# Expert pairs of a transformer layer: lags of 3, 6 and 9 steps in place of 2, 4 and 6

## The chip, the cores and the metric

The kernel runs on one core of one Trainium2 chip, as one program. The metric is device time in microseconds (us) from the start to the end of the program. A core has five engines with queues of their own: TensorE (PE; its weight loads are PEld), VectorE (DVE), ScalarE (ACT), GpSimd (POOL) and SyncE (SP), which here only issues DMAs. Engines meet at semaphores: an instruction raises a count, another waits for it.

## The reference

One layer on 8 sequences of 512 tokens, width 256, in float32. The routed part is computed densely in the reference; the kernel sorts tokens by expert.

```
x = x + attention(layernorm(x))          # 16 query heads, 4 key heads, rotary, causal
h = layernorm(x)
logits = h @ gate_w.T                    # 64 experts
topv, topi = top_k(logits, 8);  rw = softmax(topv)
gate, up = split(h @ gu_w[e].T)          # 256 -> 2 x 64, for each expert e
out = sum over chosen e of  rw[e] * (silu(gate) * up) @ dp_w[e].T      # 64 -> 256
out = out + sigmoid(h @ sh_gate1_w.T) * ((silu(h @ sh_gate_w.T) * (h @ sh_up_w.T)) @ sh_down_w.T)
x = x + out
```

## The kernel before

The first stage makes attention, the second layernorm and the routing, and scatters every token's row to `rows_d` once for each of its 8 experts, so that the rows of an expert lie in blocks of 128 (320 blocks, the last never used). The second stage, which the change touches, takes the blocks in 160 pairs (`PAIRS`). It is software-pipelined by hand: each engine runs through one loop over `STEPS` steps, and in step i it does different stages of different pairs:

- SyncE loads the rows of a pair into `xg` (L1155), up to eight pairs ahead.
- TensorE turns the rows, `turn_x` (L1402, into PSUM `psA`); ScalarE copies them to `xT` (L1297).
- GATE steps later TensorE multiplies by the expert's gate and up weights, `gate_up` (L1412, `psB`), found by a register from the list of block owners; ScalarE makes silu of the gate half into `inner` (L1302) and VectorE multiplies the up half in (`gated`, L1216).
- TURN steps after its rows were turned, the pair's inner rows are turned, `turn_inner` (L1420, `psC`); ScalarE copies them to `innerT` (L1306).
- DOWN steps after, the down product, `down` (L1429, `psD`); ScalarE copies it to `y` (L1313) and GpSimd scatters its two blocks to `res_d` with two indirect DMAs (L1497), to the rows that VectorE has worked out in `dst_i` (`pick` and `destine`).

A step's order on TensorE is down, shared products, turn_inner, then a count up of `e_front`; gate_up, turn_x, then a count up of `e_back`. ScalarE's is y copy, innerT copy (both wait for `e_front` of that step), silu, xT copy (both wait for `e_back`). VectorE's is the product, then every second step the destinations of two pairs, then sums.

The buffers are rings: `xT`, `inner` and `innerT` hold A = 3 pairs, `xg` holds 16 blocks, `y` 10 blocks, `dst_i` 32 blocks, and each of psA to psD two pairs. `down` waits until psD's bank has been copied (`e_d`) and for its innerT (`e_c`); `gate_up` waits for xT (`e_a`), `turn_inner` for inner (`e_in`).

`SOONER` lists the steps of the first two pairs, which are not delayed by the full lag. Beside the pairs, each 128-token tile is summed over its 8 expert rows once all its blocks are scattered: SyncE waits for the scatters and loads `yk` and `xs` (`load_tile`, at a turn given by LOADED_BEFORE), VectorE adds from step `sum_step` on (SUMMED_AFTER), and TensorE, at fixed steps after `sum_step`, makes the shared expert. The last four tiles are summed after the loop, from loads that wait for the last scatter (L1174).

Of the kernel before, what the change touches and what calls it, by code (L numbers as in the profile page):

```python
# [56 lines left out]
def build(nc, x, const, wqkv, wo, wroute, wgu, wdp, wshd, out):  # L57
# [7 lines left out]
    with ExitStack() as top:  # L65
# [919 lines left out]
        with ExitStack() as ctx:  # L985
# [2 lines left out]
            held_back = sb("held_back", [P, EXPERTS * D], F32)  # L988
            PAIRS = BLOCKS // 2
            G, R, Y, A = 16, 4, 10, 3  # L990
            GATE, TURN, DOWN = 2, 4, 6
            xg = sb("xg", [P, G, ROW], F32)
            xT = sb("xT", [P, A, 2, KC, P], F32)
            inner = sb("inner", [P, A, 2, P], F32)
# [35 lines left out]
            res_v = res_d.rearrange("(t p k) h -> t p (k h)", p=P, k=TOP)  # L1030

            STEPS = PAIRS + DOWN + 4
            SOONER = {GATE: (1, 2), TURN: (2, 4), DOWN: (3, 6)}
            step_of = {stage: [SOONER[stage][i] if i < 2 else i + stage for i in range(PAIRS)] for stage in SOONER}

            def pairs_at(stage, step):

                return [i for i in range(PAIRS) if step_of[stage][i] == step]
            LOADED_BEFORE, SUMMED_AFTER = 26, 12
            SUM_STEPS, TURN_SHARED, DOWN_SHARED, MIX = 4, 2, 4, 5  # L1040


            def held_of(pair):

                return min(2, USED - 2 * pair)
# [331 lines left out]
            def _(pe):  # L1377
# [19 lines left out]
                def turn_x(i):  # L1397

                    pe.wait_ge(e_x[i % (G // 2)], 16 * (2 * i // G + 1))
                    for b in range(held_of(i)):  # L1400
                        for c in range(KC):
                            last = pe.transpose(psA[:, i % 2, (b * KC + c) * P:(b * KC + c + 1) * P],  # L1402
                                                xg[:, (2 * i + b) % G, c * P:(c + 1) * P], ident)
                    return last

                def gate_up(i):

                    pe.wait_ge(e_a, i + 1)
                    for b in range(held_of(i)):
                        off = offsets[2 * i + b]  # L1410
                        for c in range(KC):
                            last = pe.matmul(psB[:, i % 2, b * GU:(b + 1) * GU], xT[:, i % A, b, c, :],  # L1412
                                             wgu_s[:, bass.ds(off + c * GU, GU)], start=(c == 0), stop=(c == KC - 1))
                    return last

                def turn_inner(i):

                    pe.wait_ge(e_in, i + 1)
                    for b in range(held_of(i)):
                        last = pe.transpose(psC[:, i % 2, b * P:(b + 1) * P], inner[:, i % A, b, :], ident)  # L1420
                    return last
# [20 lines left out]
                for i in range(STEPS):  # L1442
                    if i % 2 == 0 and i < PAIRS:
                        load_offsets(2 * i)
                    for pair in pairs_at(DOWN, i):
                        last = down(pair)
                    for tile, s in tile_at(i):
                        if s == DOWN_SHARED:
                            pe.wait_ge(c_t, tile + 1)
                    for tile, s in tile_at(i - 1):  # L1450
                        if s == MIX:
                            pe.wait_ge(c_mix, tile + 1)
                    for tile, s in tile_at(i):
                        if s == TURN_SHARED:
                            last = turn_shared(tile)
                        if s == DOWN_SHARED:
                            last = down_shared(tile)
                    for pair in pairs_at(TURN, i):
                        last = turn_inner(pair)
                    if has_front(i):  # L1460
                        last.then_inc(e_front, 1)
                    for pair in pairs_at(GATE, i):
                        last = gate_up(pair)
                    if i < PAIRS:
                        last = turn_x(i)
                    if has_back(i):
                        last.then_inc(e_back, 1)
# [91 lines left out]
```

## Time and profile before

| what | value |
|---|---|
| median of 3 runs | 1210.2 us (1207.94 to 1212.99) |
| span of the profiled execution | 1382.2 us |
| its own time beside the span | the profile tells none |
| mean granted clock of TensorE | 0.909 of 2.4 GHz |
| TensorE, VectorE, ScalarE, GpSimd busy | 1080.5, 703.8, 647.6, 722.5 us |
| expert stage | about 809 to 1355 us of the span |

The profiled execution is slower than the others by 172.0 us; times inside it are on its own scale. In a row, a group of instructions is named by line, engine, operation, and what it writes and reads; "waited for" rows give the total wait, how many times, and the longest.

### The profile page before, as it was taken

The numbers are of one execution on the slowest core, as the hardware profiler recorded it, in microseconds if no ns is written. First come the engines' busy times: TensorE is split into PE (matmuls) and PEld (weight loads), VectorE is DVE, ScalarE is ACT, GpSimd is POOL, SyncE is SP. The second block draws the span as 40 slices with busy tenths as digits, with TensorE's granted clock in tenths as the row PEclk, the third lists the DMA queues.
The fourth block names the chain that finished last, engine by engine and source line by source line (L and its number), as shares of the span: only waits on it lengthen the run. The fifth ranks groups of instructions, "written<-read, shape, count | busy, mean of one in ns | idle before, by whom it ended". The sixth has DMA issues, their size and how long they took to land.

```text
span 1382.2 us, 23533 instructions
## 1 busy us (share of the span) xinstructions
PE 1080.5 (78%) x7305; PEld 833.1 (60%) x7305; DVE 703.8 (51%) x2197; ACT 647.6 (47%) x1586; POOL 722.5 (52%) x953
## 2 busy tenths in 40 slices
PE   3799998888888888889765058887888878787875
PEld 1566666565565656566534047777777767676763
DVE  3476766666666666656525411121245544444447
ACT  2465656555555555655331024444445444444441
POOL 3111225657466564564566735655565565655552
PEclk9699999999999989989877569999999999998996
DMA  2586877212122121122228855555767777776536
GB/s 82 174 288 221 275 256 237 101 48 95 51 84 93 53 90 51 59 102 61 84 93 289 269 172 161 172 169 154 238 233 251 268 268 248 259 243 238 170 138 212
DMA packets 142824, 233.18 MB, mean 169 GB/s; under 512 B 17303, under 2 KB 119910, under 8 KB 137840
## 3 DMA queue, kind: packets, MB, share of 16 engines
q1 hardware_dynamic: 67936, 101.06, 22.7%
q0 software_dynamic: 27600, 69.28, 14.1%
q10 hardware_dynamic: 47168, 61.35, 13.5%
q8 instruction: 63, 1.03, 0.3%
q14 instruction: 57, 0.47, 0.1%
HBM read 107.32 MB, written 132.53 MB: 174 GB/s over the span
## 4 chain that ended last, share of the span: by engine, by line
PE 46%; DVE 16%; another core or an unknown queue 14%; issue 13%; ACT 8%; POOL 1%; DMA 1%; ACTq 0%; SPq 0%; DVEq 0%; POOLq 0%
PE psB L1412 6%; DVE nmax L868 6%; PE psD L1429 5%; PE psv L607 4%; PE ps L511 4%; PE psA L1402 4%; PE ps L558 3%; PE ps L518 3%; PE psp L490 3%; PE psp L504 3%; PE psC L1420 3%; ACT xT L1297 2%; ACT y L1313 2%; PE psq L634 2%
## 5 line engine op out<-in xcount | busy, mean ns | idle before, releaser
L1497 POOL DMA_INDIRECT res_d<-y,dst_i x319 | 320.9, 1006 | 231.9 <-ACT y L1313 117.8
L463 POOL DMA_INDIRECT rows_d<-pay,slot_i x256 | 256.5, 1002 | 75.4 <-issue 73.4
L868 DVE TENSOR_REDUCE nmax<-ps 128x1 f32<-128x512 f32 (+3 forms) x448 | 225.8, 531 | 135.8 <-PE ps L518 93.5
L736 ACT ACTIVATE wgu_s<-ps 128x512 f32<-128x512 f32 x320 | 191.9, 600 | 123.4 <-PE ps L518 91.3
L1216 DVE TENSOR_TENSOR inner<-inner,psB 128x128 f32<-128x128 f32 x160 | 45.8, 286 | 316.8 <-ACT inner L1302 250.5
L1429 PE MATMUL psD<-wdp_s,innerT 128*128 x638 | 174.8, 397 | 21.1 <-ACT innerT L1306 17.6
L1412 PE MATMUL psB<-wgu_s,xT 128*128 x1276 | 179.1, 285 | 1.2 <-ACT xT L1297 0.8
L518 PE MATMUL ps<-mask,ident_b 128*128 128x256 bf16 (+1 forms) x640 | 175.4, 274 | 0.4 <-issue 0.4
L511 PE MATMUL ps<-kT,qT 96*128 96x512 f32 (+3 forms) x512 | 168.3, 391 | 8.1 <-DVE nmax L868 4.8
L558 PE MATMUL ps<-qT,kT 128*128 128x512 f32 (+3 forms) x512 | 165.8, 387 | 4.9 <-ACT wgu_s L736 4.2
L1412 PEld LDWEIGHTS psB<-wgu_s,xT 128*128 128x128 f32 x1276 | 163.9, 201 | 1.8 <-issue 1.2
L1313 ACT COPY y<-psD 128x512 f32<-128x512 f32 x160 | 97.7, 610 | 110.1 <-PE psC L1420 53.7
L1402 PE MATMUL psA<-cst,xg 128*128 128x128 f32 x638 | 102.9, 284 | 55.2 <-DMA xg<-rows_d 51.2
L1429 PEld LDWEIGHTS psD<-wdp_s,innerT 128*128 128x128 f32 x638 | 113.7, 199 | 37.4 <-issue 27.9
L1302 ACT ACTIVATE inner<-psB 128x128 f32<-128x128 f32 x160 | 48.6, 304 | 176.9 <-remote 106.0
L1297 ACT COPY xT<-psA 128x512 f32<-128x512 f32 x160 | 97.6, 610 | 56.0 <-PE psA L1402 56.0
L1402 PEld LDWEIGHTS psA<-cst,xg 128*128 128x128 f32 x638 | 80.0, 148 | 57.3 <-DMA xg<-rows_d 52.1
L511 PEld LDWEIGHTS ps<-kT,qT 96*128 96x128 f32 x512 | 90.0, 205 | 32.7 <-DVE nmax L868 16.3
L518 PEld LDWEIGHTS ps<-mask,ident_b 128*128 128x128 bf16 x640 | 64.4, 101 | 65.9 <-issue 37.4
L1243 DVE SCALAR_TENSOR_TENSOR acc<-yk,rw_all,acc 128x256 f32<-128x256 f32 x202 | 97.7, 483 | 5.0 <-DMA yk<-res_d 0.7
L1420 PE MATMUL psC<-cst,inner 128*128 128x128 f32 x319 | 64.8, 286 | 41.8 <-DVE inner L1216 33.9
L558 PEld LDWEIGHTS ps<-qT,kT 128*128 128x128 f32 x512 | 91.5, 206 | 7.9 <-ACT wgu_s L736 4.6
(256 smaller groups left out, 1620.0 us busy)
## 6 DMA issues: line engine op xcount, KB each, us to landing
rows_d<-blank ACTq DMA_DIRECT2D x8, 5440.0 KB, 19.3
xg<-rows_d SPq DMA_DIRECT2D x160, 272.0 KB
yk<-res_d SPq DMA_DIRECT2D x28, 1024.0 KB
wgu_s<-wgu_in ACTq DMA_DIRECT2D x8, 1024.0 KB
x_d<-x SPq DMA_DIRECT2D x30, 192.5 KB
xs<-x_d SPq DMA_DIRECT2D x30, 192.5 KB, 2.5
res_d<-y,dst_i POOLq DMA_INDIRECT x319
wgu_s<-x_in SPq DMA_DIRECT2D x32, 128.0 KB, 2.2
```

What stands on the lines that cost most here:

```text
L463: pool.indirect_dma_start(rows_d, bass.IndirectOffsetOnAxis(ap=slot_i[par][:, t, k:k + 1], axis=0), pay[par][:, t, :], None).then_inc(s_sc ...
L511: pe.matmul(ps1[:, bank, at:at + keys], qT[par][0:96, p, i * P:(i + 1) * P], kT[par][0:96, 2 * (p // 2) + ab, 0:keys], start=(at == 0), st ...
L518: return pe.matmul(blocks, ident_b[:], mask[:].unsqueeze(1).to_broadcast([P, blocks.shape[1], P]), start=False, stop=True, skip_group_chec ...
L558: pe.matmul(ps2[:, bank, at:at + n], kT[par][:, 2 * (p // 2) + ab, kt * P:(kt + 1) * P], qT[par][:, p, kt * P:SEQ], start=(at == 0), stop= ...
L736: act.activation(pexp[p % 4][:, s, :], ps2[:, (5 * p + s) % 2, :], ACT.Exp, scale=HEAD_D ** -0.5).then_inc(s_exp, 1)
L868: return dve.tensor_reduce(nmax[u][:, tile, heads[0]:heads[-1] + 1], src, AX.X, ALU.max, negate=True)
L1297: act.copy(xT[:, i % A], psA[:, i % 2, :].rearrange("p (b k n) -> p b k n", b=2, k=KC)).then_inc(e_a, 1)
L1313: act.copy(y[:, 2 * i % Y:2 * i % Y + 2, :].rearrange("p b h -> p (b h)"), psD[:, i % 2, :]).then_inc(e_d, 1)
L1402: last = pe.transpose(psA[:, i % 2, (b * KC + c) * P:(b * KC + c + 1) * P], xg[:, (2 * i + b) % G, c * P:(c + 1) * P], ident)
L1412: last = pe.matmul(psB[:, i % 2, b * GU:(b + 1) * GU], xT[:, i % A, b, c, :], wgu_s[:, bass.ds(off + c * GU, GU)], start=(c == 0), stop=(c ...
L1429: last = pe.matmul(psD[:, i % 2, b * D:(b + 1) * D], innerT[:, i % A, b, :], wdp_s[:, bass.ds(off, D)], start=True, stop=True)
L1497: pool.indirect_dma_start(res_d, bass.IndirectOffsetOnAxis(ap=dst_i[:, j % (2 * G):j % (2 * G) + 1], axis=0), y[:, j % Y, :], None, bounds ...
```

## The change

The three lags grow by half: gate and up runs 3 steps behind the turning of the rows, the turning of the inner rows 6, and the down product 9. The first pairs' steps, the number of steps, and the turns of the loads and the sums move along. With lags of three, the two PSUM banks are no longer guarded by waits that are there anyhow, so TensorE gets three more waits: turn_x until the xT copy of two pairs before has read psA, gate_up until the product of two pairs before has read psB, turn_inner until the innerT copy of two pairs before has read psC.

```diff
-            GATE, TURN, DOWN = 2, 4, 6
+            GATE, TURN, DOWN = 3, 6, 9
...
-            SOONER = {GATE: (1, 2), TURN: (2, 4), DOWN: (3, 6)}
+            SOONER = {GATE: (1, 3), TURN: (2, 5), DOWN: (3, 7)}
...
-            LOADED_BEFORE, SUMMED_AFTER = 26, 12
+            LOADED_BEFORE, SUMMED_AFTER = 32, 15
...
                 def turn_x(i):
 
                     pe.wait_ge(e_x[i % (G // 2)], 16 * (2 * i // G + 1))
+                    if i >= 2:
+                        pe.wait_ge(e_a, i - 1)
...
                 def gate_up(i):
 
                     pe.wait_ge(e_a, i + 1)
+                    if i >= 2:
+                        pe.wait_ge(e_in, i - 1)
...
                 def turn_inner(i):
 
                     pe.wait_ge(e_in, i + 1)
+                    if i >= 2:
+                        pe.wait_ge(e_c, i - 1)
```

## Rows read from the trace of the kernel before

**Rows 1.** The page: its first line, and the chain by engine.
```profile
span 1382.2 us, 23533 instructions
...
PE 46%; DVE 16%; another core or an unknown queue 14%; issue 13%; ACT 8%; POOL 1%; DMA 1%; ACTq 0%; SPq 0%; DVEq 0%; POOLq 0%
```

**Rows 2.** Stretches: length, busy PE, PEld, DVE, ACT, POOL, granted clock, DMA share, GB/s.
```profile
809.00:820.10 11.10, 9.60 (x38) 8.34 (x39) 2.61 (x14) 4.33 (x8) 0.00 (x0) 0.50 0.74 230
...
1001.00:1355.00 354.00, 286.27 (x1900) 248.50 (x1898) 174.01 (x596) 166.33 (x490) 211.87 (x209) 0.96 0.67 232
```

**Rows 3.** The chain by line, from 809 to 1361 us.
```profile
by line: another core or an unknown queue 23.4%; PE psB L1412 14.1%; PE psD L1429 12.3%; issue 9.3%; PE psA L1402 9.0%; PE psC L1420 6.9%; ACT xT L1297 4.1%; ACT y L1313 4.0%; ACT innerT L1306 3.3%; DVE acc L1243 2.7%; ACT inner L1302 2.1%;
```

**Rows 4.** Timeline of TensorE in one step (start, us).
```profile
829.37 1.03 PE L1429 MATMUL psD<-wdp_s,innerT 128*128 x4
830.24 0.38 PE L1420 MATMUL psC<-cst,inner 128*128 128x128 f32 x2
830.46 1.06 PE L1412 MATMUL psB<-wgu_s,xT 128*128 x8
831.35 0.60 PE L1402 MATMUL psA<-cst,xg 128*128 128x128 f32 x4
831.79 1.03 PE L1429 MATMUL psD<-wdp_s,innerT 128*128 x4
```

**Rows 5.** Timeline of GpSimd at the same place.
```profile
829.86 0.98 POOL L1497 DMA_INDIRECT res_d<-y,dst_i  x1 [1.95 <-ACT y L1313]
831.15 0.98 POOL L1497 DMA_INDIRECT res_d<-y,dst_i  x1 [0.30 <-issue]
```

**Rows 6.** Waits of TensorE, 809 to 1361 us.
```profile
PE psA L1402 <- DMA xg<-rows_d: 51.2, 1, 51.2
PE psC L1420 <- DVE inner L1216: 33.9, 15, 4.2
PE psD L1429 <- ACT innerT L1306: 17.6, 18, 2.1
PE psC L1435 <- DVE fin L1257: 15.7, 13, 3.9
```

**Rows 7.** Timeline of TensorE and ScalarE around one longer wait.
```profile
833.76 0.60 PE L1402 MATMUL psA<-cst,xg 128*128 128x128 f32 x4
833.96 0.38 ACT L1306 COPY innerT<-psC 128x256 f32<-128x256 f32 x1
838.54 0.28 ACT L1302 ACTIVATE inner<-psB 128x128 f32<-128x128 f32 x1 [4.21 <-remote]
839.19 0.44 PE L1420 MATMUL psC<-cst,inner 128*128 128x128 f32 x2 [1.55 <-DVE inner L1216]
```

**Rows 8.** Waits of ScalarE and of SyncE's queue without a known releaser.
```profile
ACT inner L1302 <- remote: 106.0, 31, 6.3
ACT y L1313 <- remote: 45.2, 20, 3.6
SPq L1155 <- remote: 100.2, 28, 7.7
```

**Rows 9.** Timeline of ScalarE's two copies in one step.
```profile
830.66 0.59 ACT L1313 COPY y<-psD 128x512 f32<-128x512 f32 x1 [0.33 <-PE psC L1420]
831.14 0.38 ACT L1306 COPY innerT<-psC 128x256 f32<-128x256 f32 x1
```

**Rows 10.** Waits of GpSimd, 809 to 1361 us.
```profile
POOL res_d L1497 <- ACT y L1313: 117.8, 47, 13.7
```

**Rows 11.** Timeline of the end: the last scatter and the loads behind it.
```profile
1359.04 0.98 POOL L1497 DMA_INDIRECT res_d<-y,dst_i  x1 [0.30 <-issue]
...
1360.19 0.32 SPq L1168 DMA_DIRECT2D xs<-x_d  x1
1361.28 1.77 SPq L1174 DMA_DIRECT2D yk<-res_d  x4
```

**Rows 12.** TensorE's queue: the second wait of the down product.
```profile
L1426 PEldq EVENT_SEMAPHORE  x158: 51/51/51, 825.4 to 1351.5; - x158
```

## The prediction

> **What bounds the kernel now.** I read the head of the page and its chain first, then the stretches, then the stage that the change touches. The profiled execution's span is 1382.2 us [rows 1]; the page shows no time around it, so span and time are one number here. It is 172.0 us over the 1210.2 us median of the runs shown. The chain gives 14.0% of the span, 193.5 us, to "another core or an unknown queue" [rows 1], and one core has no other core. So the profiled execution holds waits that may not be in the timed runs, and the prediction has to say which.
>
> The expert stage runs from 809 to about 1355 us [rows 2]. In it the chain runs through TensorE's four products (14.1, 12.3, 9.0 and 6.9%) and through 23.4% of unknown releases [rows 3]: of the 552 us window, 129 us. The reader is to see that the stage has two nearly equal limits once those are set aside:
>
> - TensorE. An undisturbed step runs from one down product to the next in 831.79 - 829.37 = 2.42 us: down 0.87, turning of inner rows 0.22, gate and up 0.89, turning of rows 0.44, with no gap [rows 4]. 160 pairs make 387 us.
> - GpSimd. Scatters start 1.29 us apart (829.86, 831.15), so a pair takes 2.58 us [rows 5], 413 us for 160 pairs. That is slower than TensorE's bare step; from step 59 on TensorE has the shared expert as well and the two come about level.
>
> TensorE's own waits in the stage that the change could touch are two: on VectorE's product before L1420, 33.9 us in 15, and on ScalarE's innerT copy before L1429, 17.6 us in 18 [rows 6]. The 51.2 us before L1402 are the wait for the first rows, ahead of the stage.
>
> Where do the two come from? At 833.96 ScalarE starts the innerT copy, at 838.54 the next silu, after 4.21 us idle "remote"; TensorE, whose row turn that silu waits for was drawn at 833.76, works on and stops only for the last 1.55 us, before 839.19 [rows 7]. ScalarE has 106.0 us of such silu waits and 45.2 us at the y copy; SyncE's row loads, which wait for the same count, have 100.2 us [rows 8]. The count that TensorE raises is seen late by both. 193.5 us of unknown chain against 172.0 us by which this execution is too long: I take these waits as mostly the profiled execution's own. That is a choice, not a reading.
>
> **The change, part by part.** All 160 pairs get the same 18 matmuls of the trace, four ScalarE and one VectorE, two scatters; nothing is added to a DMA. What moves is when.
>
> *How far TensorE may run ahead.* xT, inner and innerT have three buffers, but psA to psD have two, and the new waits guard those. Step by step: before, the down product of step s needs the y copy and the innerT copy of step s-2, the inner turning needs the product of step s-2, and gate needs the xT copy of step s-2. After, down needs the y copy of step s-2, the inner turning the innerT copy of s-2 (its buffer), gate the product of s-2, the row turning the xT copy of s-2. The lead stays two steps. Each wait moves behind one more piece of work: the wait on the product behind an inner turning, 0.22 us; the wait on the innerT copy behind a down product, but the y copy of the same ScalarE step still holds that, and it ends at 831.25 against 831.52 for the innerT copy [rows 9], so 0.27 us. Relief at most 15 x 0.22 + 18 x 0.27 = 3.3 + 4.9 = 8.2 us, and only where those waits exist. For the timed runs I take 0, the end nearer to a step that shows no gap [rows 4]; 8.2 stays for the range.
>
> *Fill.* The first two pairs are hurried through; the steady stream of scatters starts with pair 2, whose down moves from step 8 to step 11. Counted off the code, ahead of it stand 11 row turnings instead of 8, 8 gates instead of 6, 5 inner turnings instead of 4: 3 x 0.44 + 2 x 0.89 + 0.22 = 3.32 us later. That costs only if GpSimd sets the pace all the way (it waited 117.8 us for y in the profiled execution [rows 10], so there it did not). At the clock of 0.50 that the first 11 us have [rows 2], twice as much, 6.64 us, at most.
>
> *Drain.* If TensorE sets the pace, its total work and its end stay. But at the start of step 160, nine pairs instead of six still have their down product to come. That moment comes 3 x 0.87 + 2 x 0.22 + 0.89 = 3.94 us sooner, and GpSimd then has three pairs more: 3 x 2.58 = 7.74. In the drain TensorE makes a pair in 0.87 to 1.98 us, so GpSimd is what ends: 7.74 - 3.94 = 3.80 us later. What hangs on it: after the last scatter (1359.04) SyncE issues the last tiles' loads at 1361.28, and these end the kernel [rows 11]. Cover: the last sums on VectorE, whose xs load is issued at 1360.19, end almost level, but one more tile's sums also fall into the drain, so I count no cover. From 0 to 3.80; I take 3.80.
>
> *Waits.* Three more per step for TensorE, 158 x 3 of them. The one extra wait that stands alone today, L1426, takes 51 ns [rows 12], in a step whose matmuls show no gap [rows 4]. Hidden, I take 0; exposed it would be 158 x 3 x 0.051 = 24.2 us.
>
> *Sums, loads, destinations.* LOADED_BEFORE and SUMMED_AFTER move by the three steps that DOWN moves, so SyncE's queue (row loads behind the wait for scatters, then yk and xs), the shared products and mix keep their places relative to the down products. One place tightens: the ring of destinations. VectorE at step i waits for the scatter of pair i-14, whose down was eight steps back and is now five; behind it stand the sums and the next product. ScalarE's y copy of that step waits for the same scatter through the ten y buffers, so it adds nothing: 0.
>
> The sum: fill or drain, not both (one pace-setter at a time): 3.32 or 3.80 us, less 0 relief. On the profiled execution, with up to 8.2 us of relief, 1382.2 + 3.8 - 8.2 = 1377.8 to 1386.0; on the median 1210.2 + 3.8 = 1214.0 us.
>
> One rule speaks against my choice of 0 relief. The rows show 193.5 us of unknown waits [rows 1] in a run that is 172.0 us too long, so they look like the cost of being profiled. The Trainium skill, "NOTIFIC — the notification-queue block", section 10, says that emitting an implicit record costs the engine zero cycles; by that the waits would be the kernel's own and the relief would count in full.
>
> **Rivals.**
>
> *The waits are the kernel's own.* Then the timed runs have them too and gain up to 8.2 - 3.8 = 4.4 us: 1205.8. For it: the waits are at ScalarE and SyncE alike, with a plain lateness of a count. Against: 172.0 us have to be somewhere else then. To pass 0.5% the relief must exceed 9.9 us, more than I can count, so it would need waits on VectorE's fin (15.7 us [rows 6]) to shrink as well.
>
> *Both ends cost (slower).* GpSimd sets the pace in the first steps, TensorE in the later ones: 3.32 + 3.80 = 7.1 us, 1217.3, and with the fill at the low clock 10.4 us, 1220.6. It decides once GpSimd is five pairs behind (12.9 us) before step 59; at 2.58 against 2.42 it loses 0.16 a step, 9.4 us by then, so not quite.
>
> *The waits cost on TensorE's queue:* 24.2 + 3.8, 1238. Rows 4 and 12 speak against it.
>
> *It does nothing:* the lead is the same two steps and the last sums cover the drain: 1210.2.
>
> **How the numbers follow.** A measurement of this kernel tells about 0.5%, 6.05 us, from no change. The forecast (drain or fill alone) 0.50, of which 0.08 is large enough to pass +0.5%; nothing 0.12; the waits its own 0.18, of which 0.10 passes -0.5%; both ends 0.15; the waits on the queue 0.05. So faster 0.10, same 0.42 + 0.12 + 0.08 = 0.62, slower 0.08 + 0.15 + 0.05 = 0.28. The range goes from 1204 (the first rival at its bound) to 1220 (both ends); the forecast's own is 1211 to 1217.
>
> **What would show it.** Undisturbed steps stay at 2.42 us; the wait before L1420 turns into one at gate (L1412) on inner, a little shorter, and that before L1429 into one on y or at the inner turning on innerT; the unknown share of the chain stays near 14%; the first stream of scatters starts some 3 us later; the last scatter comes later after TensorE's last down product. It is wrong if steps get shorter in the mean by more than 0.05 us (the lead was worth more than counted), or if gaps appear at the new waits.

## The result, and the profile after

The changed kernel takes 1214.4 us (median of 20 runs, 1211.2 to 1217.5), the kernel before 1210.3 us (20 runs) on the same chip: ratio 1.0035, 95% interval 1.0025 to 1.0045. It is 4.2 us slower, inside the half per cent that was called "no change", and 0.4 us from the forecast. The sum came out; which of its two terms had been paid did not, as the rows show, so that its closeness is luck.

Two kernels are compared below: the changed one, and the kernel before profiled a second time ("before again"), since the first profile of it, that of [rows 1 to 12], turned out to be an unusual execution. First the page of the changed kernel: its first line, the tenths in which PE (TensorE) and POOL (GpSimd) were busy, and the chain.

```profile
span 1215.1 us, 24006 instructions
PE   3699988998989888989998610999999999999985
POOL 3111122774765847747467776377777777777772
PE 14%; DMA 9%; issue 7%; POOL 6%; ACT 2%; DVE 1%; POOLq 0%; ACTq 0%; DVEq 0%; SPq 0%
```

And of before again, the first line and the chain:

```profile
span 1208.9 us, 23533 instructions
PE 15%; issue 7%; DMA 7%; POOL 7%; DVE 2%; ACT 1%; POOLq 0%; SPq 0%; ACTq 0%; DVEq 0%
```

"Another core or an unknown queue", 14% in [rows 1], is in neither chain. Both chains are traced back only over the expert stage, some 40% of the span; but neither span stands above the range of the timed runs, so there is no room for such waits ahead of it either, and no later profile gives a wait to "remote", as [rows 8] do. The 193.5 us belonged to that one execution. With them gone, most of TensorE's waits of [rows 6] and ScalarE's of [rows 8] are gone too.

What is left shows who sets the pace of the expert stage. In the tenths PE has its nines there, but POOL's sevens, from the 27th slice on, are the fuller engine: 0.98 us of every 1.29 us is counted busy, and the 0.30 us between two scatters is called "issue". A POOL at 7 is a POOL without a gap. The chain doesn't settle the matter: it gives TensorE more than GpSimd (14 and 15% here), because TensorE has hardly any idle time in this stage either (busy 392 of the 413 us from 781 to 1194). What settles it is the experiment with a padded GpSimd, below. GpSimd's scatters at the start of the stage and at its end, changed kernel (start, duration, and in brackets the idle time before with its releaser):

```profile
767.39 1.00 POOL L1503 DMA_INDIRECT res_d<-y,dst_i  x1 [12.24 <-ACT y L1313]
774.54 0.98 POOL L1503 DMA_INDIRECT res_d<-y,dst_i  x1 [4.85 <-ACT y L1313]
781.66 0.98 POOL L1503 DMA_INDIRECT res_d<-y,dst_i  x1 [4.84 <-ACT y L1313]
782.95 0.98 POOL L1503 DMA_INDIRECT res_d<-y,dst_i  x1 [0.30 <-issue]
...
1193.58 1.02 POOL L1503 DMA_INDIRECT res_d<-y,dst_i  x1 [0.30 <-issue]
```

The same of before again:

```profile
767.55 1.00 POOL L1497 DMA_INDIRECT res_d<-y,dst_i  x1 [13.65 <-ACT y L1313]
771.86 0.98 POOL L1497 DMA_INDIRECT res_d<-y,dst_i  x1 [2.02 <-ACT y L1313]
775.88 0.98 POOL L1497 DMA_INDIRECT res_d<-y,dst_i  x1 [1.75 <-ACT y L1313]
...
1187.71 1.05 POOL L1497 DMA_INDIRECT res_d<-y,dst_i  x1 [0.30 <-issue]
```

The two scatters of pair 2 begin at 781.66 and 775.88. From there to the last one, 314 intervals on, none is longer than 1.55 us in either kernel: (1193.58 - 781.66) / 314 = 1.312 us, and (1187.71 - 775.88) / 314 = 1.312 us. In these two profiles nothing inside the stream differs. What differs is when it starts. The first row turning, changed kernel and then before again:

```profile
757.09 1.11 PE L1404 MATMUL psA<-cst,xg 128*128 128x128 f32 x4 [52.03 <-DMA xg<-rows_d]
```

```profile
755.72 1.12 PE L1402 MATMUL psA<-cst,xg 128*128 128x128 f32 x4 [51.85 <-DMA xg<-rows_d]
```

Counted from there, the stream starts after 781.66 - 757.09 = 24.57 us in the changed kernel and after 775.88 - 755.72 = 20.16 us in before again: 4.41 us later, and the time is 4.2 us longer. The very first scatter even comes sooner (10.30 against 11.83 us), but the third and the fifth wait 4.85 and 4.84 us where they waited 2.02 and 1.75.

### The profile page after: what moved, and what is told of

Same layout as the page of the kernel before. It is cut to its first block and busy times, and to the rows that moved or that the text cites. A ratio compares the mean times of both kernels' runs of the same rounds, so it can differ in the third digit from the quotient of the medians.

```text
span 1215.1 us, 24006 instructions
## 1 busy us (share of the span) xinstructions
PE 1030.2 (85%) x7305; PEld 812.6 (67%) x7305; DVE 706.3 (58%) x2197; ACT 656.5 (54%) x1586; POOL 721.6 (59%) x953
## 3 DMA queue, kind: packets, MB, share of 16 engines
q10 hardware_dynamic: 47168, 61.35, 15.3%
## 5 line engine op out<-in xcount | busy, mean ns | idle before, releaser
L1435 PE MATMUL psD<-wdp_s,innerT 128*128 x638 | 166.7, 384 | 7.0 <-ACT y L1313 4.0
L1416 PE MATMUL psB<-wgu_s,xT 128*128 x1276 | 171.2, 278 | 0.8 <-ACT xT L1297 0.8
L1416 PEld LDWEIGHTS psB<-wgu_s,xT 128*128 128x128 f32 x1276 | 156.9, 193 | 1.9 <-issue 1.2
L1313 ACT COPY y<-psD 128x512 f32<-128x512 f32 x160 | 94.1, 588 | 116.1 <-DMA res_d<-y,dst_i 78.9
L1404 PE MATMUL psA<-cst,xg 128*128 128x128 f32 x638 | 97.6, 277 | 52.0 <-DMA xg<-rows_d 52.0
L1297 ACT COPY xT<-psA 128x512 f32<-128x512 f32 x160 | 94.2, 590 | 55.3 <-PE psA L1404 55.3
L1435 PEld LDWEIGHTS psD<-wdp_s,innerT 128*128 128x128 f32 x638 | 109.7, 192 | 17.0 <-issue 8.6
L1404 PEld LDWEIGHTS psA<-cst,xg 128*128 128x128 f32 x638 | 76.8, 144 | 53.0 <-DMA xg<-rows_d 53.0
L607 PE MATMUL psv<-wgu_s 128*32 128x512 f32 (+3 forms) x1024 | 82.8, 442 | 0.7 <-ACT wgu_s L736 0.7
L421 POOL TENSOR_SCALAR rstd<-mv 128x1 f32<-128x1 f32 x32 | 7.6, 237 | 117.7 <-DVE mv L825 116.3
```

What stands on the lines that cost most here:

```text
L1313: act.copy(y[:, 2 * i % Y:2 * i % Y + 2, :].rearrange("p b h -> p (b h)"), psD[:, i % 2, :]).then_inc(e_d, 1)
L1435: last = pe.matmul(psD[:, i % 2, b * D:(b + 1) * D], innerT[:, i % A, b, :], wdp_s[:, bass.ds(off, D)], start=True, stop=True)
```

## The experiments

Each is read by the same measure: the start of pair 2's first scatter after the first row turning, less the 20.16 us of before again ("shift", from one profile each), beside the change of the time ((ratio - 1) x 1210 us). From pair 2's first scatter to the last one it is 410.3 us (slow fill) to 413.8 us (215 turnings ahead) in the single profiles of these runs, so a shift and a change can be held against each other to some 2 us, not closer.

| run | shift, us | ratio (95%) | change, us |
|---|---|---|---|
| changed kernel | +4.41 | 1.0035 (1.0025 to 1.0045) | +4.2 |
| quick fill, long lags | +0.47 | 0.9995 (0.9984 to 1.0007) | -0.6 |
| slow fill, short lags | +4.24 | 1.0029 (1.0015 to 1.0043) | +3.5 |
| three waits only | +0.22 | 0.9995 (0.9983 to 1.0007) | -0.6 |
| lags 1, 2, 3 | -2.76 | 0.9967 (0.9951 to 0.9983) | -4.0 |
| late stream | +6.35 | 1.0046 (1.0028 to 1.0064) | +5.6 |
| hurried fill | -3.05 (+3.55 in two gaps) | 0.9990 (0.9978 to 1.0002) | -1.2 |
| 56 turnings ahead | +0.73 | 0.9998 (0.9986 to 1.0009) | -0.2 |
| the same, lags 1, 2, 3 | -2.47 | 0.9982 (0.9969 to 0.9994) | -2.2 |
| 215 turnings ahead | -3.91 | 0.9975 (0.9962 to 0.9988) | -3.0 |
| the same, lags 1, 2, 3 | -6.80 | 0.9946 (0.9929 to 0.9964) | -6.5 |

**Before again.** The kernel before, unchanged.

> The kernel before, unchanged, for a profile of it to lay beside the one after (where GpSimd's scatters run without a gap over 1.6 us from pair 2, 781.66 us, to the last, 24.57 us after the first row turning at 757.09). Time within 0.3% of 1210.3 us by every theory. Fill theory (GpSimd sets the pace from pair 2 to the last scatter): the scatters run without gaps here too, over some 412 us, and start about 21 us after the first row turning, 3.3 to 4 us sooner than after. Drain theory (TensorE sets the pace): GpSimd waits for y again and again in the middle, and the last scatter follows the last down product by some 4 us less than the 10.8 us of after.

1212.0 us, ratio 1.0005 (0.9991 to 1.0019), profile above. The unknown waits don't come back, so they are no fixed part of the kernel.

**Quick fill, long lags.** The changed kernel with the first 40 pairs at the old lags and the old SOONER; its drain and all steps after pair 40 are the changed kernel's.

```
EARLY = {GATE: 2, TURN: 4, DOWN: 6}
step_of = {stage: [SOONER[stage][i] if i < 2 else i + (EARLY[stage] if i < 40 else stage)
...
```

> The kernel after, but the first 40 pairs run at the lags 2, 4 and 6 with the first two pairs' steps of before, and the lags grow to 3, 6 and 9 from pair 40 on, so only the fill is undone; the three waits and everything late are as after. Fill theory: back to before, 1210 to 1211.5 us (ratio 0.999 to 1.001). Drain theory: as after, 1214 us (1.003). Theory that the three waits cost: 1214 us.

```profile
756.16 1.11 PE L1406 MATMUL psA<-cst,xg 128*128 128x128 f32 x4 [51.70 <-DMA xg<-rows_d]
776.79 0.98 POOL L1505 DMA_INDIRECT res_d<-y,dst_i  x1 [1.75 <-ACT y L1315]
```

The start is back at 776.79 - 756.16 = 20.63 us, and the loss is gone with the long drain still there. The lags grow at pair 40 without leaving a gap: no interval of this stream passes 1.53 us.

**Slow fill, short lags.** The reverse: the changed kernel's start and its three waits; between pairs 30 and 42 the lags shrink to 2, 4 and 6, and the end is that of before.

```
GATE, TURN, DOWN = 2, 4, 6
SOONER = {GATE: (1, 3), TURN: (2, 5), DOWN: (3, 7)}
SHORTER_AT = {GATE: (42,), TURN: (36, 38), DOWN: (30, 32, 42)}
...  i + stage + sum(i < at for at in SHORTER_AT[stage])
```

> The other half: the fill of the kernel after (lags 3, 6 and 9 and the three waits), brought back to the lags 2, 4 and 6 one by one between pairs 30 and 42, with the turns of loads and sums of before, so the drain is that of before. Fill theory: 1213.5 to 1215 us (1.003 to 1.004). Drain theory: 1210 us (1.000). Waits theory: 1214 us.

```profile
756.19 1.11 PE L1406 MATMUL psA<-cst,xg 128*128 128x128 f32 x4 [51.91 <-DMA xg<-rows_d]
780.59 0.98 POOL L1505 DMA_INDIRECT res_d<-y,dst_i  x1 [4.84 <-ACT y L1315]
```

A start of 24.40 us and nearly the whole loss, with the drain of before. The two runs together leave the fill as the cause and the drain as nothing.

**Three waits only.** The kernel before with the change's three waits and no other lag.

```
+ if i >= 2: pe.wait_ge(e_a, i - 1)     (turn_x)
+ if i >= 2: pe.wait_ge(e_in, i - 1)    (gate_up)
+ if i >= 2: pe.wait_ge(e_c, i - 1)     (turn_inner)
```

> The kernel before with the three added waits alone, which are always met by then. Fill and drain theories: 1210.3 us (0.999 to 1.001). Waits theory: 1214 us (1.003), up to 24 us more if the 51 ns of each were exposed.

No cost that can be measured: an interval of -2.1 to +0.8 us, where 24.2 had been the bound.

**Padded GpSimd.** Does GpSimd set the pace throughout? The kernel before with a memset of an unused 128x256 tile ahead of every fourth scatter, 80 in all.

```
+ if j % 4 == 0:
+     if j:
+         pool.wait_ge(e_pad, j // 4)
+     pool.memset(pool_pad[:], 0.0).then_inc(e_pad, 1)
```

> The kernel before with one fill of a 128x256 scratch tile ahead of every fourth scatter on GpSimd, 80 in all, some 0.31 us each as that size took before the stage, and a little issue time. It touches nothing that others wait for but GpSimd's own pace. If GpSimd sets the pace from pair 2 to the last scatter: 25 to 31 us longer, 1236 to 1241 us (1.021 to 1.026). If TensorE sets the pace and GpSimd only ends the drain: 0 to 3 us.

1223.0 us, ratio 1.0106 (1.0083 to 1.0128): 12.8 us, half of what was expected of the pace-setter. The rows of one pad:

```profile
901.73 0.99 POOL L1503 DMA_INDIRECT res_d<-y,dst_i  x1 [0.30 <-issue]
902.70 0.35 POOL L1502 MEMSET pool_pad<- 128x256 f32 x1
903.21 0.99 POOL L1503 DMA_INDIRECT res_d<-y,dst_i  x1 [0.17 <-POOL pool_pad L1502]
```

The next scatter starts 1.48 us after the last instead of 1.29: the memset lies mostly in the 0.30 us that pass anyway and adds 0.19. The mean interval of the stream is 1.355 us instead of 1.312, and 314 x 0.043 = 13.5 us, which the measured 12.8 us agrees with (10.0 to 15.5). The price of a pad was wrong; the pace is GpSimd's, as TensorE's work is the same and the time grew by all that GpSimd's stream did.

**Lags 1, 2, 3.** If the start decides, shorter lags than before must gain; if a long lead protects TensorE, they must lose.

```
GATE, TURN, DOWN = 1, 2, 3
SOONER = {GATE: (1, 2), TURN: (2, 3), DOWN: (3, 4)}
LOADED_BEFORE, SUMMED_AFTER = 20, 9
```

> The kernel before with the lags 1, 2 and 3 throughout, the turns of loads and sums three steps sooner to match, and none of the added waits. Fill theory (only the start of the steady scatters counts): pair 2 is scattered 15.5 to 17.5 us after the first row turning in place of 20.2, so 2.7 to 4.7 us shorter, 1206 to 1208.5 us (0.996 to 0.998). Theory that the lead of several steps is worth something: with one step between a product and its use TensorE waits in the steps that carry sums, its step passes the 2.62 us that a pair takes on GpSimd, and the time is over 1212 us.

```profile
756.23 1.12 PE L1402 MATMUL psA<-cst,xg 128*128 128x128 f32 x4 [52.08 <-DMA xg<-rows_d]
773.63 0.99 POOL L1497 DMA_INDIRECT res_d<-y,dst_i  x1 [0.30 <-issue]
```

Pair 2's first scatter follows pair 1 without a wait (773.63), 17.40 us after the first turning, and the kernel is 4.0 us faster. No interval of the stream passes 1.55 us, and TensorE waits for innerT five times, 4.0 us together. The lead of the long lags is worth nothing here.

**Late stream.** The stream alone held up: 16 memsets on GpSimd, one by one, ahead of pair 2's first scatter, in the kernel before.

```
+ if j == 4:
+     for n in range(16):
+         pool.memset(pool_pad[:], 0.0).then_inc(e_pad, 1)
+         pool.wait_ge(e_pad, n + 1)
```

> The kernel before (lags 2, 4 and 6) with 16 fills of a scratch tile on GpSimd, one after the other, ahead of pair 2's first scatter alone; TensorE's fill and drain are untouched. The fills take 0.35 us each and a little for the wait, 6.5 to 8 us, of which GpSimd's own idle time there (1.75 us) takes a part, so the steady scatters start 4.7 to 6.3 us later. Fill theory: the time moves by that, 1215 to 1216.6 us (1.004 to 1.005), though no lag is changed. Drain theory, or TensorE as the pace: 1210.3 us (1.000), since ten y buffers take up the delay.

```profile
758.73 1.11 PE L1404 MATMUL psA<-cst,xg 128*128 128x128 f32 x4 [52.54 <-DMA xg<-rows_d]
778.63 5.84 POOL L1501 MEMSET pool_pad<- 128x256 f32 x16 [1.03 <-ACT y L1315]
785.24 0.98 POOL L1503 DMA_INDIRECT res_d<-y,dst_i  x1 [0.78 <-POOL pool_pad L1501]
```

The start is at 785.24 - 758.73 = 26.51 us, 6.35 us later, and the kernel is 5.6 us slower (3.4 to 7.7), with TensorE's order untouched. So the start of the scatters by itself costs almost its full length.

**Hurried fill.** Lags 1, 2, 3 for the first pairs, grown one by one to 2, 4, 6, with the three waits, to keep both a quick start and the lead.

```
SOONER = {GATE: (1, 2), TURN: (2, 3), DOWN: (3, 4)}
LONGER_AT = {GATE: (36,), TURN: (16, 26), DOWN: (12, 22, 32)}
...  i + stage - sum(i < at for at in LONGER_AT[stage])
```

> The lags 1, 2 and 3 for the first pairs alone, grown one by one to 2, 4 and 6 between pairs 12 and 36, ten pairs apart for the down product, so that GpSimd has scatters in hand when a step without a down product comes; with the three added waits. Everything from pair 36 on is as before. Fill theory: as the lags 1, 2 and 3 throughout or a little better, 1206 to 1208.5 us (0.996 to 0.998). Lead theory: the same here, since the sums only begin at step 59. Drain theory: 1210.3 us (1.000).

1210.1 us: a miss. The start came 3.05 us sooner, but the first two of the three steps at which DOWN grows, steps in which no down product is made, run GpSimd dry:

```profile
796.62 0.98 POOL L1505 DMA_INDIRECT res_d<-y,dst_i  x1 [0.30 <-issue]
799.62 0.98 POOL L1505 DMA_INDIRECT res_d<-y,dst_i  x1 [2.02 <-ACT y L1315]
...
824.13 0.98 POOL L1505 DMA_INDIRECT res_d<-y,dst_i  x1 [0.30 <-issue]
827.26 0.98 POOL L1505 DMA_INDIRECT res_d<-y,dst_i  x1 [2.14 <-ACT y L1315]
```

These intervals take 3.00 and 3.13 us instead of 1.29, together 3.55 us, a little more than had been won. Measured are -1.2 us (-2.7 to +0.2), no gain that can be told from none.

**56 turnings ahead, two runs.** The first 11 us of the stage run at a clock of 0.50 [rows 2]. TensorE turns the identity 56 times while it waits for the rows, once GpSimd has counted up; the results go to a PSUM bank that is free then. The second run has lags 1, 2, 3 as well.

```
+ if ending(h, par, 1) and n == TILES * TOP - 6: pool.sem_inc(e_warm)
...
+ pe.wait_ge(e_warm, 1)
+ for n in range(56): pe.transpose(psB[:, 1, 0:P], ident, ident)
```

> The kernel before with 56 idle turnings of the identity on TensorE, into a bank that is free then, from some 12 us before the first rows come in, so that its clock is not at 0.50 for the first 10 us of the fill. Fill theory: TensorE's 8.6 us of work at the low clock take half of that, so the steady scatters start 17 us or less after the first row turning in place of 20.2, and the time falls by some 3 to 4.3 us, 1206 to 1207.5 us (0.9965 to 0.9975). Drain theory: 1210.3 us (1.000), as the end is GpSimd's last scatters behind TensorE's last down products only if TensorE, not the start, sets when these come; a sooner start would then move the whole stage as well, so this run tells whether the low clock costs, and the runs before it tell the theories apart.

> The same idle turnings with the lags 1, 2 and 3 throughout. Fill theory: both gains add, since both only bring the steady scatters forward: 7 to 8 us shorter than before, 1202.5 to 1204 us (0.9935 to 0.995). If the stage has another limit just below, such as the loads of the first rows or TensorE's steps, less than 5 us.

Both missed (0.9998 and 0.9982). The turnings ran far too soon:

```profile
728.13 8.44 PE L1391 MATMUL psB<-cst 128*128 128x128 f32 x56 [24.93 <-POOLq L464]
755.12 1.11 PE L1408 MATMUL psA<-cst,xg 128*128 128x128 f32 x4 [18.55 <-DMA xg<-rows_d]
```

Then TensorE was idle for 18.55 us. By windows (stretch, length, busy PE, PEld, DVE, ACT, POOL, granted clock, DMA share, GB/s) the clock had risen during the turnings and was back at half when the stage began:

```profile
732.00:736.00 4.00, 4.00 (x36) 4.00 (x36) 0.00 (x0) 0.00 (x0) 3.05 (x4) 0.93 0.28 104
744.00:755.00 11.00, 0.00 (x0) 0.00 (x0) 0.00 (x0) 0.00 (x0) 6.17 (x8) 0.50 0.36 121
755.00:766.70 11.70, 10.07 (x41) 8.81 (x42) 2.62 (x14) 4.52 (x9) 0.00 (x0) 0.50 0.70 221
```

**215 turnings ahead, two runs.** The same edit with `range(215)`, so that the turnings last until the rows come.

> As the run with 56 idle turnings, but 215 of them: those began 27 us before the first row turning and ended 18.55 us before it, so that the clock had fallen back; 215 end some 1.4 us before it. The granted clock should then be 1.00 through the fill. If the low clock of the fill costs: the steady scatters start some 16 to 17.5 us after the first row turning in place of 20.2, and by the fill theory the time falls by 2.7 to 4.2 us, 1206 to 1207.5 us (0.9965 to 0.998). If the first scatters hang on ScalarE's copies and on the DMAs of the first rows more than on TensorE's clock: less than 1.5 us, 1209 to 1210.3 us.

> The 215 idle turnings with the lags 1, 2 and 3 throughout. If both gains count and add: 6 to 8 us shorter than before, 1202.5 to 1204.5 us (0.9935 to 0.9955). If GpSimd is no longer the pace once it starts sooner, or the first rows' loads hold the start: between 1205 and 1207.5 us, as the lags 1, 2 and 3 alone.

First the run with the old lags, then the first window of the run with lags 1, 2, 3:

```profile
727.64 26.51 PE L1391 MATMUL psB<-cst 128*128 128x128 f32 x215 [25.74 <-POOLq L464]
754.62 0.66 PE L1408 MATMUL psA<-cst,xg 128*128 128x128 f32 x4 [0.47 <-DMA xg<-rows_d]
770.87 0.98 POOL L1503 DMA_INDIRECT res_d<-y,dst_i  x1 [1.75 <-ACT y L1316]
```

```profile
754.00:765.00 11.00, 8.89 (x66) 7.78 (x67) 2.90 (x15) 6.22 (x13) 1.91 (x2) 1.00 0.87 280
```

The clock is at 1.00 from the first row turning on (0.66 us instead of 1.11), the stream starts 16.25 us after it instead of 20.16, and the ratio is 0.9975. Of the 3.91 us some 1.0 us is given back in the profiled execution by two intervals of 1.96 and 1.65 us, at 951 to 956 us, where GpSimd ran dry once for 0.96 us; why is open. With lags 1, 2, 3 the start is at 13.36 us and the time 1203.8 us, ratio 0.9946 (0.9929 to 0.9964): faster than both kernels; by the two ratios, 10.8 us faster than the changed one.

## Why the prediction came out as it did

**The unknown waits** were taken as "mostly the profiled execution's own", as a choice. It holds: none in before again, none after. Why that execution had them stays open. The rule put against it is that emitting an implicit record costs the engine zero cycles (the Trainium skill, "NOTIFIC — the notification-queue block", section 10). Nothing in these runs speaks against it: the profiled execution of before again took 1210.7 us, where the median of its twelve runs is 1212.0; whether an execution without any records is faster, no run here shows. What failed was the step from that rule to "the waits are the kernel's own".

**Relief 0, waits 0, undisturbed step 2.42 us**: as forecast. The step in the changed kernel:

```profile
836.89 1.03 PE L1435 MATMUL psD<-wdp_s,innerT 128*128 x4
...
839.31 1.03 PE L1435 MATMUL psD<-wdp_s,innerT 128*128 x4
```

839.31 - 836.89 = 2.42 us, as in [rows 4]. The waits that were to wander had almost nothing to wander: without the unknown waits, TensorE's wait for inner is 0.7 us in 1 in before again (33.9 in 15 in [rows 6]), and the one for innerT 3.0 us in 2 (17.6 in 18). After the change the latter is gone and one on y is there, 4.0 us in 3, as was said. Of the other signs, the later start of the stream came; the unknown share of the chain did not stay near 14%, and the last scatter did not come later after the last down product.

**The step that failed: who sets the pace.** "It waited 117.8 us for y, so there it did not" was read in an execution in which ScalarE's copies of y were late for a reason of that execution. GpSimd's waits for y in before again (total, times, longest):

```profile
POOL res_d L1497 <- ACT y L1313: 28.7, 40, 13.6
```

Of the 28.7 us, 13.65, 2.02 and 1.75 are the three shown above, and the other 37, 0.30 us each, are the gap that stands between two scatters anyway. That wrong reading chose the drain of 3.80 us for the sum and put the fill aside, although the same rows gave GpSimd 413 us and TensorE's bare steps 387. The runs show the reverse: fill paid nearly in full (slow fill, late stream), drain not measurably (quick fill). That 1214.0 was met within half a microsecond is luck: 3.80 us for a term that cost nothing is near the 4.41 us of the one that was put aside.

**Why the drain was nothing.** GpSimd's stream has no gap from pair 2 on, so its end follows from its start; TensorE's lead only changes how long a block lies in y. From the last down product's end to the last scatter's end it is 10.8 us after the change and 12.0 in before again, where 3.8 more had been forecast. The last down product, after and before again:

```profile
1182.62 1.19 PE L1435 MATMUL psD<-wdp_s,innerT 128*128 x2 [2.97 <-issue]
```

```profile
1176.07 0.67 PE L1429 MATMUL psD<-wdp_s,innerT 128*128 x2 [1.06 <-DVE fin L1257]
```

(1183.81 to 1194.60; 1176.74 to 1188.76.) From the code: y holds 10 blocks, so the down product can run 10 x 1.29 = 12.9 us ahead of the scatters whatever the lags are. ScalarE's copies of y waited for a scatter to land, after and in before again:

```profile
ACT y L1313 <- DMA res_d<-y,dst_i: 78.9, 62, 4.6
```

```profile
ACT y L1313 <- DMA res_d<-y,dst_i: 59.0, 43, 4.9
```

This fits a longer lead of TensorE that ends at the full ring; that the ring is the reason was argued, not tried with a longer ring.

**The fill, sized 3.32 us, measured 4.41.** The windows from the first row turning to pair 2's down product (same columns as above), changed kernel and then before again:

```profile
757.09:768.50 11.41, 9.91 (x40) 8.69 (x41) 1.68 (x9) 4.17 (x7) 1.00 (x1) 0.50 0.71 222
768.50:778.95 10.45, 10.29 (x88) 9.95 (x87) 4.33 (x22) 6.71 (x18) 2.96 (x3) 1.00 0.73 207
```

```profile
755.72:765.80 10.08, 8.58 (x34) 7.51 (x35) 2.52 (x14) 3.75 (x7) 0.00 (x0) 0.50 0.71 227
765.80:773.18 7.38, 7.38 (x63) 7.14 (x63) 1.61 (x8) 4.75 (x12) 3.01 (x4) 1.00 0.66 186
```

If work at a clock of 0.50 counts half, TensorE does 9.91/2 + 10.29 = 15.25 us at the full clock against 8.58/2 + 7.38 = 11.67, by this estimate: 3.58 us more, where 3.32 had been counted. The count of the steps was right (11, 8 and 5 operations stand ahead of pair 2's down product in the trace), only their size was a little larger. A further 1.33 us of busy time at half the clock, which costs 0.67 on top of its work, and 0.16 us more of idle time make 4.41. The bound of 6.64 us supposed that all of the added work would run at half; the clock had risen before most of it.

The clock of 0.50, 1.2 of 2.4 GHz, follows 52 us in which TensorE did nothing but wait for the rows; with turnings through the last 27 us ahead of the rows it is 1.00 from the start. The Trainium skill ("TensorE: Matmul & The Clock Gate", "What's actually happening") says that "the default state is throttled, and activity releases the throttle", and these two clocks agree with it.

**The rivals.** That the unknown waits are the kernel's own fell with before again, and that the added waits cost on TensorE's queue fell with three waits only. "Both ends cost" had the right half: GpSimd behind from the first steps on.

## What to carry to other kernels

In a pipeline whose last engine works without a gap, one more step of lag costs the work that it puts ahead of that engine's first steady item, once, and buys nothing as long as that engine never waits for its input afterwards. Shorter lags are the better choice until they make it wait, as two steps without a down product did in the hurried fill. Find that engine by the intervals between the starts of its instructions, not by its busy share: here GpSimd at 7 tenths was full. Then add a little work to that engine alone and see whether the time grows by as much. And before an argument rests on the waits of one profile, hold its span against the timed runs; where it stands well above them, every wait downstream of the disturbance is suspect.

## What the runs showed of the hardware

- A 128x256 memset on GpSimd, 0.35 us by itself, adds only 0.19 us between two scatters.
- A count that stands in GpSimd's program ahead of a scatter can be raised long before that scatter runs. In the run with 56 turnings it stood ahead of the sixth scatter from the end, and TensorE was released by it at 728.13:

```profile
743.42 0.96 POOL L466 DMA_INDIRECT rows_d<-pay,slot_i  x1 [0.30 <-issue]
...
749.74 0.96 POOL L466 DMA_INDIRECT rows_d<-pay,slot_i  x1 [0.30 <-issue]
```

  The last scatter starts at 749.74 and the sixth from the end at 743.42, so the count came 15.3 us ahead of it. Such a count did not tell TensorE when the scatter ran.
- A clock that has risen is lost again within a wait: in the 8.4 us of turnings it rose (0.93 from 732 to 736), then TensorE was idle for 18.55 us, and the stage began at 0.50 as if there had been none.
